# One level of Strassen's scheme in a float32 linear layer with per-sequence LoRA and residual

## The reference

```python
# x (32, 128, 2048) float32, 32 sequences of 128 rows; ids (32,), values 6 to 15
# W (2048 out, 2048 in), bias (2048), A (32 adapters, 16, 2048), B (32, 2048, 16)
h      = einsum('bsd,brd->bsr', x, A[ids])            # (32, 128, 16)
result = einsum('bsd,od->bso', x, W) + bias
result = result + einsum('bsr,bor->bso', h, B[ids])
return x + result
```

## Time and profile before

| | |
|---|---|
| median of 3 runs (range) | 1510.79 us (1509.51 to 1511.89) |
| profiled execution: span | 1511.0 us |
| instructions | 19950 |
| TensorE / DVE / ACT / POOL busy | 1490.4 / 392.7 / 282.4 / 173.5 us |
| DMA | 173.16 MB, mean 115 GB/s |

### The profile page before, as it was taken

One profiled execution on the slowest core, in us unless ns is written; L12 is line 12 of the kernel. 1 busy time (PEld: TensorE's weight loads), 2 busy tenths in 40 slices (PEclk: granted clock), 3 DMA queues, 4 the chain that ended last, 5 costly groups with the idle time before them and its releaser, 6 DMA issues.

```text
span 1511.0 us, 19950 instructions
## 1 busy us (share of the span) xinstructions
PE 1490.4 (99%) x7872; PEld 1349.8 (89%) x7872; DVE 392.7 (26%) x576; ACT 282.4 (19%) x449; POOL 173.5 (11%) x135
## 2 busy tenths in 40 slices
PE   6999999999999999999999999999999999999998
PEld 6999999999999999999988888888888888888887
DVE  5422222222222222222253222222222222222221
ACT  4211211112111121111251111111111111111110
POOL 0201101011010110101101110110110110110110
PEclk9999999999999999999999999999999999999999
DMA  9423233232332323323283233232232232232230
GB/s 327 138 89 130 82 117 109 89 131 84 114 112 86 132 87 111 113 85 131 91 300 127 83 125 104 83 125 104 83 125 104 84 124 100 88 125 98 89 123 30
DMA packets 43099, 173.16 MB, mean 115 GB/s; under 512 B 4562, under 2 KB 8658, under 8 KB 35282
## 3 DMA queue, kind: packets, MB, share of 16 engines
q1 hardware_dynamic: 43090, 173.03, 33.4%
HBM read 139.46 MB, written 33.55 MB: 115 GB/s over the span
## 4 chain that ended last, share of the span: by engine, by line
PE 96%; DMA 2%; DVE 1%; SPq 1%; issue 0%; ACT 0%; DVEq 0%
PE acc L603 47%; PE acc L503 32%; PE acc L514 15%; PE acc L563 2%; DMA a_raw<-aT 1%; DMA b_raw<-bT 1%; DVE w_lo L377 0%; DMA out<-res 0%; DVE res L403 0%; SPq L161 0%; PE turned L551 0%; SPq L167 0%; SPq L177 0%; DVE b_stack L387 0%; ACT b_stack L292 0%
## 5 line engine op out<-in xcount | busy, mean ns | idle before, releaser
L503 PE MATMUL acc<-w_hi,x_hi 128*128 128x352 f32 x1536 | 334.6, 326 | 14.0 <-ACT w_hi L280 8.5
L503 PE MATMUL acc<-w_hi,x_lo 128*128 128x352 f32 x1536 | 332.0, 324 | 0.0
L603 PE MATMUL acc<-w_lo,x_hi 128*128 128x512 f32 x1024 | 321.8, 395 | 0.0
L603 PE MATMUL acc<-w_hi,x_hi 128*128 128x512 f32 x1024 | 320.3, 393 | 0.0
L603 PE MATMUL acc<-w_hi,x_lo 128*128 128x512 f32 x1024 | 320.1, 393 | 0.0
L514 PE MATMUL acc<-w_lo,x_hi 128*128 128x352 f32 (+1 forms) x1536 | 293.5, 321 | 0.0
L503 PEld LDWEIGHTS acc<-w_hi,x_hi 128*128 128x128 f32 x1536 | 261.2, 190 | 15.0 <-DVE w_hi L382 12.4
L503 PEld LDWEIGHTS acc<-w_hi,x_lo 128*128 128x128 f32 x1536 | 264.0, 190 | 0.0
L276 ACT ACTIVATE x_hi<-x_raw 128x512 fp32r<-128x512 f32 x256 | 158.8, 628 | 537.6 <-PE acc L603 344.8
L514 PEld LDWEIGHTS acc<-w_lo,x_hi 128*128 128x128 f32 x1536 | 252.1, 190 | 0.3 <-DVE w_lo L377 0.3
L372 DVE TENSOR_TENSOR x_lo<-x_raw,x_hi 128x512 fp32r<-128x512 f32 x256 | 175.9, 707 | 233.6 <-ACT x_hi L276 231.7
(11 more groups left out here) (17 smaller groups left out, 149.6 us busy)
## 6 DMA issues: line engine op xcount, KB each, us to landing
x_raw<-xT SPq DMA_DIRECT2D x60, 1024.0 KB, 5.1
res<-x SPq DMA_DIRECT2D x64, 512.0 KB, 3.7
out<-res SPq DMA_DIRECT2D x64, 512.0 KB, 4.5
w_raw<-wT SPq DMA_DIRECT2D x32, 512.0 KB, 11.4
b_raw<-bT SPq DMA_DIRECT2D x64, 256.0 KB
x_raw<-xT SPq DMA_DIRECT2D x16, 256.0 KB, 11.7
a_raw<-aT SPq DMA_DIRECT2D x32, 128.0 KB, 2.7
bias_sb<-bias SPq DMA_DIRECT2D x1, 1024.0 KB, 19.1
```

The source lines that it names most:

```text
L503: mm = nc.tensor.matmul(acc[j][:, o, 0:COLS_A], xs, w_hi[:, k, base + o * COLS_A:base + (o + 1) * COLS_A], start=(k == 0 and part == 0), s ...
L603: mm = nc.tensor.matmul(acc[j][:, o], xs, ws[:, k, at0 + o * BANK:at0 + (o + 1) * BANK], start=(k == 0 and n == 0), stop=False)
```

## The change

x is cut into two row halves (sequences 0 to 15, and 16 to 31) and two input halves (chunks 0 to 7, and 8 to 15), W into two by two blocks. Instead of eight block products there are seven, each a *phase* of 16 tiles of 8 chunks. In the order P1, P2, P6, P5, P4, P7, P3:

| phase | x side | W side | columns of A | B, bias | output side |
|---|---|---|---|---|---|
| P1 | x11 | W11 | yes | | kept in SBUF (`keep`) |
| P2 | x12 | W12 | yes, late h | yes | residual + P1 + P2 stored |
| P6 | x21+x22-x11 | a sum | | | added to `keep` |
| P5 | x21+x22 | a sum | yes | | + `keep` + two residuals, two stores to DRAM (`u4`) |
| P4 | x22 | a sum | yes, late h | yes | residual and P4 into `keep` |
| P7 | x11-x21 | a sum | | yes | into `keep` and `u4[0]`, two stores |
| P3 | x12-x21-x22+x11 | W22 | | yes | into `u4[1]`, stored |

POOL builds the sums of x in place (`sum_x`), and during P1 also the four sums of W blocks, which go through DRAM (`prep_load`, `prep`, `prep_store`). W has 12 chunk slots: 4 chunks of the next phase are loaded during the last two pairs of tiles, 4 more when the last tile has used its first four chunks. x_hi and x_lo are double by tile, b_stack and h_stack single. h of the phases P2 and P4 is the sum of two phases' parts and is reused in P3 and P7. The bias is a row of B's stack.

```diff
-GROUPS = 4
-SWEEPS = 2
+SLOTS = 12
+AHEAD = SLOTS - KC            # KC = 8 chunks, TILES = 16, PAIRS = 8
+P1, P2, P6, P5, P4, P7, P3 = PHASES = range(7)
+H_PHASES = (P1, P2, P5, P4)
+LORA_PHASES = (P2, P4, P7, P3)
+LATE_PHASES = (P2, P4)
+MORE_AT = {P6: ((4, 5), (4, 5)), P5: ((6,), (6,)), P7: ((3,), (5,)), P3: ((3, 5, 6), (3, 5, 6))}
+OUT_AT = {P2: ((6,), (2,)), P5: ((2, 3), (4, 5)), P4: ((2,), (4,)), P7: ((2,), (4,)), P3: ((2,), (4,))}
...
+            def load_x(tile):                                            # sync
+                sp.wait_ge(x_lo_done, x_count(tile) - 2)
+                sp.dma_start(x_raw(j), block_of(tile, MAIN[ph])).then_inc(pool_in[j], DMA)
...
+                back = len(MORE[ph]) if ph == P7 else 0
+                    sp.wait_ge(x_summed, sums_by(tile) - back)
+                for (_, which), b in zip(MORE[ph], MORE_AT[ph][j]):
+                    sp.dma_start(pool[:, b], block_of(tile, which)).then_inc(pool_in[b], DMA)
...
+            def step(tile):                                              # sync
+                if two.ph < len(PHASES):
+                    load_x(two)
+                    if two.ph in H_PHASES:
+                        load_a(two)
+                if ph == P1:
+                    if j == 0:
+                        prep_load(i)       # four loads, each waits for the store of its buffer
+                    else:
+                        prep_store(i)      # waits for all four sums
+                if not (ph == P1 and is_first(tile)):
+                    store(after(tile, -1))
+                if one.ph < len(PHASES):
+                    load_out(one)          # waits for the store of its buffer
+                    if one.ph in LORA_PHASES:
...
+                        load_b(one)
+                if is_last(tile) and one.ph < len(PHASES):
+                    load_w_rest(one.ph)    # each waits for chunk_used of the last tile
...
+            def step(tile):                                              # scalar
+                    b_high(tile)
+                    x_high(one)
+                        a_high(one)
+                if known and i >= PEELED and ph + 1 < len(PHASES):
+                    w_high(ph + 1, row(tile) - 2 * PEELED)
+                if ph in LORA_PHASES:
+                    h_high(tile)
+                    h_out(tile)
+                if is_last(tile) and ph + 1 < len(PHASES):
+                    for k in range(AHEAD, KC):
+                        w_high(ph + 1, k)
...
+            def step(tile):                                              # vector
+                    b_low(tile)
+                    x_low(one)
+                        a_low(one)
+                    w_low(ph + 1, row(tile) - 2 * PEELED)
+                if ph in LATE_PHASES:
+                    h_total(tile)
+                if ph in LORA_PHASES:
+                    h_low(tile)
+                if is_last(tile) and ph + 1 < len(PHASES):
+                    for k in range(AHEAD, KC):
+                        w_low(ph + 1, k)
+                if one.ph == P4:
+                    take_b(one)
+                read_out(tile)
...
+            def step(tile):                                              # gpsimd
+                if two.ph in SUM_PHASES:
+                    sum_x(two)
+                if two.ph == P4:
+                    take_a(two)
+                if ph == P1 and j == 1:
+                    prep(i)
+                if one.ph in ADD_PHASES:
+                    add_out(one)
...
+            def whole(tile):                                             # tensor
+                begin(tile)                # waits for x_lo, for the accumulator's reader, for a_ready
+                if ph in LATE_PHASES:
+                    for k in range(KC):
+                        mm = chunk(tile, k, normal=False)
+                    mm.then_inc(h_done, 1)
+                    pe.wait_ge(w_lo_done, KC * ph + KC)
+                    for k in range(KC):
+                        with_lo(ph, j, k, [o for o in ALL if o != H_BANK[j]])
+                    turn(tile)
+                    for k in range(KC):
+                        mm = with_lo(ph, j, k, [H_BANK[j]], after_h=True)
+                        if k < KC - AHEAD:
+                            mm.then_inc(chunk_used, 1)
+                    low_rank(tile)
+                elif ph in LORA_PHASES:
+                    for k in range(KC // 2):
+                        chunk(tile, k)
+                    turn(tile)             # waits for h_cols_ready
+                    for k in range(KC // 2, KC):
+                        chunk(tile, k)
+                    low_rank(tile)
+                else:
+                    for k in range(KC):
+                        mm = chunk(tile, k)
+                    mm.then_inc(tile_done, 1)
```

More of the change, by code:

```diff
@@ new lines, in row, with place, nth, is_first @@
+def row(tile):
+    return 2 * tile.i + tile.j
+def place(tile):
+    return TILES * tile.ph + row(tile)
+def nth(tile, phases):
+    return TILES * phases.index(tile.ph) + row(tile)
+def is_first(tile):
+    return isinstance(tile.i, int) and tile.i == 0 and tile.j == 0
+def is_last(tile):
+    return isinstance(tile.i, int) and tile.i == PAIRS - 1 and tile.j == 1
+def sums_by(tile):
+    before = TILES * sum(len(MORE[ph]) for ph in SUM_PHASES if ph < tile.ph)
+    return before + len(MORE.get(tile.ph, ())) * (row(tile) if tile.ph in SUM_PHASES else 0)
@@ L51, in pieces @@
+LOADS = [loads_before(ph) for ph in range(len(PHASES) + 1)]
+STORES = [stores_before(ph) for ph in range(len(PHASES) + 1)]
+def pieces(ph, j):
+    if ph not in H_PHASES:
+        return [(o, 0, BANK, o * BANK) for o in range(2)]
     found, out = [], 0
@@ L172, in load_b, with block_of @@
[L172 to L180, removed]
+            def block_of(tile, which):
+                rows, half = which
+                return xT[bass.ds(seq_of(tile, rows), 1), :, half * KC:(half + 1) * KC]
@@ new lines, in load_b, with rows @@
+            def load_b(tile):
+                n = nth(tile, LORA_PHASES)
+                adapter = adapter_of(seq_of(tile, 0 if tile.ph in (P2, P3) else 1))
+                if not (isinstance(n, int) and n == 0):
+                    sp.wait_ge(b_ready, n)
+                def rows(half):
+                    return bT[bass.ds(adapter, 1), :, half * HALF:(half + 1) * HALF].to_broadcast([2, RANK, HALF])
+                sp.dma_start(b_raw[0:AC], rows(0 if tile.ph in (P2, P4) else 1)).then_inc(b_in, DMA)
+                if tile.ph == P4:
+                    sp.dma_start(pool[0:AC, B2_AT], rows(1)).then_inc(pool_in[B2_AT], DMA)
@@ L204, in _ @@
[L204 to L254, removed]
@@ new lines, in a_high @@
+            def a_high(tile):
+                ph, i, j = tile
+                n = nth(tile, H_PHASES)
+                if ph == P4:
+                    act.wait_ge(a_taken, row(tile) + 1)
+                else:
+                    act.wait_ge(a_in[j], DMA * (PAIRS * H_PHASES.index(ph) + i + 1))
+                if not (isinstance(n, int) and n < 2):
+                    act.wait_ge(tile_done, place(tile) - 1)
+                runs = slot_runs(ph)
+                for s, k, m in runs:
+                    did = nc.scalar.activation(w_hi[:, s:s + m, A_AT[j]:A_AT[j] + RANK], a_raw[:, j, k:k + m], COPY)
+                did.then_inc(a_hi_done, 1)
@@ L560, in low_rank, with chunk @@
[L560 to L569 removed]
+            def chunk(tile, k, normal=True):
+                ph, _, j = tile
+                pe.wait_ge(w_hi_done, KC * ph + k + 1)
+                with_hi(ph, j, k, 0)
+                mm = with_hi(ph, j, k, 1)
+                if normal:
+                    pe.wait_ge(w_lo_done, KC * ph + k + 1)
+                    mm = with_lo(ph, j, k, ALL)
+                    if k < KC - AHEAD:
+                        mm.then_inc(chunk_used, 1)
+                return mm
@@ new lines, in turn, with low_rank @@
+            def turn(tile):
+                n = nth(tile, LORA_PHASES)
+                pe.wait_ge(h_cols_ready, n + 1)
+                if not (isinstance(n, int) and n == 0):
+                    pe.wait_ge(h_ready, n)
+                nc.tensor.matmul(turned[:, 0:ROWS], h_cols[:].rearrange("p a b -> p (a b)"), eye[:],
+                                 start=True, stop=True).then_inc(h_turned, 1)
+            def low_rank(tile):
+                ph, _, j = tile
+                n = nth(tile, LORA_PHASES)
+                pe.wait_ge(b_ready, n + 1)
+                pe.wait_ge(h_ready, n + 1)
+                for o, low, m, first in pieces(ph, j):
+                    mm = nc.tensor.matmul(acc[j][:, o, low:low + m], h_stack[:], b_stack[:, first:first + m],
+                                          start=False, stop=True,
+                                          skip_group_check=(ph in H_PHASES and o == H_BANK[j]))
+                mm.then_inc(tile_done, 1)
@@ new lines, in _ @@
+                    mm = chunk(Tile(P1, 0, j), k)
```

(10 more changed lines are left out.)

925 lines of the change are left out of this document (546 added, 379 removed).

## The result

The changed kernel takes 1562.7 us (median of 4 runs, 1560.5 to 1570.1) against 1510.2: ratio 1.036 (95% interval 1.033 to 1.039). It is slower by 3.6%, and I had forecast 1410 us, faster, with 1345 to 1480 as the range.

What follows compares the result with a forecast made beforehand. TensorE, busy 99% of the span, was taken as the bound. Work 1306 + start 14 + end 6 + P1 17 + steady tiles 5 + P7 12 + P3 18 + phase changes 34 = 1412, predicted 1410 us, range 1345 to 1480.

Steps and rivals of the forecast that it cites:

- the work terms: TensorE's own work per tile, 11.13 to 12.04 us by phase, 1306 us in all if never kept waiting.
- the port's exclusion: POOL adds and DVE splits lock each other out of the shared SBUF port; either can wait up to 2.4 us.
- So P2 starts at 216: P1's loads, W sums and stores cycle at 24.5 us a pair, delaying P2's start from 199 to 216: 17 us.
- The phase changes: Late W chunks and DVE's order delay the first tiles' turns at phase starts; with clock losses, 34 us (15 to 60).
- P7, 12 us: In P7, B's late landing leaves nothing for a POOL add before x_low: 0.8 us a tile, 12 us (0 to 35).
- P3, 18 us: In P3, three POOL sums per tile plus DVE splits take 12.8 us against 11.65: 18 us (0 to 45).
- P2 and P4, 5 us: A POOL add may delay the h handover in P2 and P4; 5 us for P2, P4, P6 and P5 (0 to 25).
- The clock, 7 us for four stalls: TensorE's granted clock falls after idling at phase changes, some 1.7 us lost each time; four stalls, 7 us.
- Rival (c): Turn over 2 us late in all 64 tiles of P2, P4, P7, P3, low clock after each; about 1620 us, chance 0.08.
- its point of decision: The loss per tile in P2, P4, P7 and P3 from which the kernel would be slower: 2.1 us.
- Its argument against: A stall of one tile lets B land earlier in the next, and P2 and P4 have h late in the tile.
- Rival (b): P1's chain and the DMA queue become the bound, at 253 GB/s for mixed traffic; about 1480 us, chance 0.11.

Runs made afterwards that it cites:

- e11: e9 with P3's sums back on POOL and, in P4, the second B half loaded once the last is subtracted: 1404.7 us, ratio 0.930.
- e14: Changed kernel with the W sums left out but for 32 of 1024 columns each (wrong results): 1509.9 us.
- e1: Changed kernel with TensorE's bias wait moved from the heads of P2, P4, P7, P3 to before the low-rank product: 1542.2 us.
- e2: Changed kernel; in P1's last tile SP issues P2's residual, bias, B and late W loads before storing the last four W sums: 1542.5 us.
- e6: Changed kernel with the edits of e1, e2 and e3 together: 1477.2 us, ratio 0.980.
- e9: Changed kernel with later bias wait, h first, P3's sums on DVE, B before residual, late W chunks issued earlier at four phase ends: 1433.2 us.
- e3: Changed kernel with h_high and h_low at the head of a tile's step in P7 and P3, before the splits: 1511.6 us.
- e4: Changed kernel with the x sums of P7 and P3 replaced by POOL memsets that read no SBUF (wrong results): 1509.7 us.
- e8: e3 with SP issuing the next tile's bias and B loads before the residual load instead of behind it: 1475.8 us.

## Why the prediction was wrong

**Right:** the work terms (P6 and P5 within 2 us, and tiles of 11.7 and 12.0 us wherever the waits were taken away, for 11.65 and 12.04 forecast); that the excess sits at P1's sums, the turns and the phase changes; the port's exclusion and splits of up to 3.4 us; the clock's drop after a gap (0.50, or 1.2 GHz, until 261 us after the gap that ended at 258). That e11, with five orders of waits and issues changed, comes to 1404.7 us is no confirmation of 1410. Its excess of 98 us lies elsewhere: P2's first tile is done at 248.1 us where 216 + 12 was forecast, and the steady tiles of P7 and P3 (11.7 us) wait for nothing where I had put 30 us.

**The steps that failed:**

- *P1: "So P2 starts at 216".* It started at 258. The first sums were stored at 42.9, not 36.5, and the cycle of W sums was 27.2 us (last stores at 233.2, not 208). From the issue of the stores to the last landing I had 13.5 us, nine transfers with one x load among them; the last such stretch took 16.4 us (207.06 to 223.51), with two x loads in it. After the last stores I put 8 us and it took 24.9: the late W chunks, then DVE's read and the bias row. e14 prices the sums at 53 us.
- *The phase changes*, 34 us. The gaps before P4 and P7 alone took 41.6 us, the one before P2 40.7. I followed the turn of the first tile, but not the wait for the bias row at the head of the phase, which I never listed. With it nothing of the first tile covers DVE's backlog of four splits, a read and the bias. e1 prices it at 20.5 us; what it left of the gaps before P2 and P4 is the wait for W's late chunks, again SP's order (e2 for P2; for P4 14.7 us in e6 and 4.6 in e9, together with other edits).
- *P7, 12 us.* It took 38.5. I wrote that nothing was left for a POOL add in front of x_low and then charged 0.8 us a tile. e3 took all waits at the turn away by order alone; freeing the port (e4) took away 20.0 of 26.5 us. About half of the excess came in the last three tiles, where the split of P3's W stands in front of h_low; I priced no such tiles.
- *P3, 18 us.* It took 60.5. I treated sums, port and B as small additions to one cycle; they were separate bounds, each of about 14 to 15 us a tile. In the tile shown, 6.95 us pass from the issue of the extras (1396.83) to the first sum, where I had 4.1, and the three sums take 9.14 us instead of 7.5: 16.1 us a cycle instead of 12.8. B was used 6.8 us after its issue (1194.24 to 1200.99 in P7), where I took 5.
- *P2 and P4, 5 us.* 32.4 us. P4's loop of two B loads is in no step of mine.
- *The clock, 7 us for four stalls.* Of the 131.4 us of excess in P2, P4, P7 and P3, 89.8 are waits at the turn; the other 41.6 are TensorE at work, but slower than forecast. The granted clock averaged 0.96 over P7 and 0.93 over P3, against 1.00 over steady sweep 1. How much of the 41.6 is the clock was not measured.

Rival (c) named the right place, the turn, and the right sign, and at 0.08 its chance was far too low. Its sizes do not hold: the wait is 1.4 us in the mean of the 64 tiles, not over 2 in all. A low clock does not follow each: it stayed at 1.00 after the 2.67 us shown above and was 0.50 after the 6.5 us in P3's first tile. The excess of the four phases, 2.05 us a tile, lies just under its point of decision, 2.1; the kernel is slower only because P1 and the gaps cost more than I had put there. Its argument against, that a late tile lets B land earlier in the next, is refuted: 28 of the 32 tiles of P7 and P3 kept a wait. That POOL's adds move with the tiles is my reading of it. Rival (b) is refuted as a bandwidth bound: e11 moves the same 297 MB in 1404 us.

Not settled is why B's loads are slow; no run varied it. The kernel before loads B in four copies, the changed kernel in two (`to_broadcast`). While hardly anything else is in flight, the DMA engines' busy share is 0.24 to 0.25 at 70 to 74 GB/s before (1108 to 1110), and 0.13 to 0.19 at 43 to 66 GB/s in e8 (948.5 to 950). That is about four and two engines of 16. If the number of copies sets it, half the bytes go over half the engines and take as long. This is a reading, not a test; another layout of this load is the experiment that is missing.

## What to carry to other kernels

When a scheme halves the work per step, price the waits by following each in-order queue for one whole step, the DMA issuer's too: a load that has nothing to do with a store's landing must not stand behind it. Chains of nearly one length hide one another, so an edit that gains nothing alone (B first, 1.5 us in P3) may be half of one that gains 47. If the forecast for a step says "nothing is left", charge the next blocker in full, not a share of it.

## What was not expected of the hardware

- A DVE subtraction on 32 columns took 2.32 us instead of 0.18 beside a POOL add. It waited 2.1 us, as long as one on 1024 columns (3.32 instead of 1.22): what counts is how often DVE meets POOL, not how much it does. Beside POOL memsets it took 0.18 us (e4).
- B's 128 KB on 32 partitions were used 6.8 us after their issue, 256 KB on 64 partitions 6.0 us after the earlier trace rows. The queue was fuller in the first case, so this is no clean comparison.
- Under a mean of 191 GB/s, x loads of 512 KB took 6.6 us in the median and the residual's 5.6; the residual's took 3.7 under 115 GB/s.
